# A three-layer decoder kernel: value products of self-attention issued 512 columns wide in every second slot

## The reference

```python
    x = x + _L0_attn_ref(_layernorm(x), W_qkv, b_qkv, W_out, b_out)
    x = x + _L0_xattn_ref(_layernorm(x), ctx_512, ...)
    x = x + _L0_ffn_ref(_layernorm(x), Wg, w1, w2)
# the part of the first that the change touches, for every batch and head (q, k: 512 x 16)
        attn = jnp.einsum('bhqd,bhkd->bhqk', q, k) / jnp.sqrt(HEAD_DIM)
        attn = jax.nn.softmax(attn, axis=-1)
        out = jnp.einsum('bhqk,bhkd->bhqd', attn, v)
```

## Time and profile before

| what | us |
|---|---|
| median of three runs | 1565.12 (1564.07 to 1566.87) |
| the profiled execution | 1563.6 |
| its span, first to last instruction | 1561.8 |
| its A units 0 to 7, from 67.19 to 502.91 | 435.72 |

### The profile page before, as it was taken

How to read it: one execution, slowest core, us unless ns; L and a number is a source line. 1 busy time by engine, 2 the same in 40 slices (tenths; PEclk the granted TensorE clock), 3 DMA queues, 4 the chain that set the end, 5 groups by cost and what they waited for, 6 DMA issues and landing times.

```text
span 1561.8 us, 37676 instructions
## 1 busy us (share of the span) xinstructions
PE 1415.5 (91%) x14538; PEld 634.1 (41%) x14538; DVE 1194.4 (76%) x2434; ACT 1055.4 (68%) x2139; POOL 653.2 (42%) x535
## 2 busy tenths in 40 slices
PE   3799999999999999999999999999899988599997
PEld 1223322332333434434334343343343432279896
DVE  6788888888877777877977878779678785547774
ACT  2387788788778677677676776776767757236562
POOL 2555574466423421336245333362353221235553
PEclk9699999999999999999999999999999999799999
DMA  6435534433323434334333332343334301167771
GB/s 180 128 117 137 147 97 124 133 115 106 94 62 104 111 88 108 91 91 107 87 93 86 105 103 64 91 109 84 84 92 109 84 21 44 42 233 259 271 243 59
DMA packets 119478, 175.80 MB, mean 113 GB/s; under 512 B 26273, under 2 KB 85895, under 8 KB 114696
## 3 DMA queue, kind: packets, MB, share of 16 engines
q1 hardware_dynamic: 111376, 158.50, 35.7%
q0 software_dynamic: 5888, 14.24, 2.8%
q10 hardware_dynamic: 2048, 0.83, 0.2%
HBM read 102.33 MB, written 51.18 MB: 98 GB/s over the span
## 4 chain that ended last, share of the span: by engine, by line
PE 58%; DVE 18%; ACT 8%; DMA 6%; issue 5%; POOL 2%; SPq 1%; DVEq 0%; POOLq 0%; ACTq 0%
PE psO L742 13%; DVE negmax L1221 11%; PE psM L467 11%; PE psS L765 10%; PE psK L467 7%; PE psK L796 6%; ACT probs L1030 6%; PE psS L467 4%; DMA stack<-mrows 3%; DMA recipB<-recip_scratch 2%; PE psK L694 2%; PE psM L832 1%; DVE xn L1169 1%; DVE mrows L1323 1%; PE psM L881 1%
## 5 line engine op out<-in xcount | busy, mean ns | idle before, releaser
L1221 DVE TENSOR_REDUCE negmax<-psS 128x1 f32<-128x512 f32 (+3 forms) x1536 | 868.8, 615 | 222.8 <-PE psS L765 113.4
L1030 ACT ACTIVATE probs<-psK 128x512 f32<-128x512 f32 (+3 forms) x1536 | 755.4, 546 | 309.6 <-PE psK L796 183.9
L742 PE MATMUL psO<-probs,V 128*32 128x256 f32 (+1 forms) x5632 | 440.3, 384 | 10.3 <-ACT U L1022 8.8
L765 PE MATMUL psS<-stack 48*128 48x512 f16 (+3 forms) x1536 | 282.6, 364 | 45.4 <-DVE negmax L1221 41.5
L796 PE MATMUL psK<-stack 50*128 50x512 f16 (+3 forms) x1536 | 276.1, 356 | 17.4 <-DMA stack<-mrows 11.4
L765 PEld LDWEIGHTS psS<-stack 48*128 48x128 f16 x1536 | 74.1, 93 | 357.0 <-DVE negmax L1221 294.9
L742 PEld LDWEIGHTS psO<-probs,V 128*32 128x32 f32 x5632 | 112.3, 108 | 192.2 <-issue 127.8
L1439 POOL TENSOR_TENSOR rstd<-lnt,minus_half 128x4 f32<-128x4 f32 x24 | 24.8, 1033 | 247.1 <-DVE lnt L1161 247.1
L796 PEld LDWEIGHTS psK<-stack 50*128 50x128 f16 x1536 | 75.9, 94 | 49.4 <-issue 17.9
L1571 POOL DMA_INDIRECT out_dram<-stack,put_to x32 | 76.8, 2399 | 17.8 <-issue 9.1
L467 PE MATMUL psM<-xT,wx 128*128 128x512 f16 x288 | 76.7, 382 | 1.6 <-DVE mrows L1323 0.6
(11 more groups left out here) (192 smaller groups left out, 2017.9 us busy)
## 6 DMA issues: line engine op xcount, KB each, us to landing
spare<-in_L_ffn_w_dram SPq DMA_DIRECT2D x32, 1024.0 KB, 6.4
parts_scratch<-parts SPq DMA_DIRECT2D x192, 128.0 KB
stack<-parts_scratch SPq DMA_DIRECT2D x96, 256.0 KB
stack<-parts_scratch SPq DMA_DIRECT2D x96, 128.0 KB
packed<-U SPq DMA_DIRECT2D x192, 64.0 KB
recipB<-recip_scratch SPq DMA_DIRECT2D x48, 256.0 KB
shared<-shared SPq DMA_DIRECT2D x48, 128.0 KB, 2.1
probs<-back_scratch POOLq DMA_DIRECT2D x16, 258.0 KB, 3.2
```

The costliest lines, as they stand in the source:

```text
L742: mm = nc.tensor.matmul(psO[32 * i:32 * i + 32, q0:q1], v_of(par)[:, kt, 2 * g + i % 2 + PAIRS * (i // 2), :], probs[:, (unit + i % 2) % P ...
L765: mm = nc.tensor.matmul(psS[:, banks[hh], 0:n], stack_of(par, 0)[rows, hp, qt * P:(qt + 1) * P], stack_of(par, 1)[rows, hp, 0:n], start=Tr ...
L1030: nc.scalar.activation(probs[:, t % P_RING, i, q0:T], psK[:, S_BANKS[t][i], q0:T], ACT.Exp, scale=SM_SCALE / (1 if b.kind == "A" else WSCA ...
L1221: nc.vector.tensor_reduce(negmax[:, g % 2, at:at + 1], psS[:, S_BANKS[u // 2][j], 0:n], AX_X, ALU.max, negate=True).then_inc(s["max_done"], 1)
```

## The change

In units of kind A, `av(t)` gives nothing in even slots, and in odd slots the whole of the key tile: columns 0 to 511. The same holds for the last groups of an A unit that fall in slots 0 to 2 of the next. `av_done` then counts 16 groups a unit in place of 32. In form "AC" the first load over the old `stack`, which had been in slot 0 and held back by the value products there, moves to slot 1, since slot 0 has none now. Kinds B and C keep the halves.

```diff
     "AC": {"v0": (0,), "v1": (2,), "ctxT0": (7,), "proj0": (10,), "proj1": (11,), "proj2": (14, 15), "proj3": (17, 18),
-           "out0": (22,), "out1": (30,), "load": (0, 3, 3, 6, 7, 9, 9, 10), "split": (8, 10, 12, 15, 18),
+           "out0": (22,), "out1": (30,), "load": (1, 3, 3, 6, 7, 9, 9, 10), "split": (8, 10, 12, 15, 18),
@@ def av(self, t):
         if not kind:
             return None
+        if kind == "A":
+            return (t < 3, (t - 3) % SLOTS, 0, T, True) if t % 2 else None
         half = (t + 1) % 2
         unit = (t - 3 - half) % SLOTS
```

## The result

| what | before | after |
|---|---|---|
| median of four runs each, us | 1565.51 (1564.07 to 1566.87) | 1579.43 (1577.03 to 1581.85) |
| the profiled execution | 1563.6 | 1581.85 |
| its span | 1561.8 | 1580.0 |
| its A units 0 to 7 | 435.7 | 455.2 (67.45 to 522.61) |
| mean granted clock of the span | 0.975 | 0.977 |

The ratio is 1.0095, 95% interval [1.007, 1.0119]: **the change makes the kernel 14 us slower**, 1579.4 where 1580 was forecast. A second series of seven runs of it gave 1.0092 [1.0059, 1.0125].

The account below looks back on a forecast made before the run. TensorE's stream bounds slots with a job, a 1.17 us floor through DVE's reduction those without. Slot pairs sum to +1.6 us a unit, all A units to +15 on the median 1565.1: 1580 us, range 1568 to 1590.

Parts of the forecast that it names:

- The floor: In A units no slot can be shorter than 1.17 us, set by a chain through DVE's reduction of the maxima.
- The rival that the saving of 0.14 a pair counts: TensorE's saving counts after all in A units, every pair of slots giving 0.14 us: 1547 us, chance 0.15.
- The wide group: A value group of 512 columns in A units takes 1.00 us to the next start, 0.43 more than 256 columns.
- the 0.144: Fixed part in us of each group of value products, from a line through groups of 128 and 256 columns.
- The rivals of a cheaper (0.93) and a dearer (1.14) wide group: 512-column value groups in A units: at 0.93 us about 1565 (chance 0.07), at 1.14 us 1598 (chance 0.04).
- The pairs: Odd slot and next even slot of an AA unit, priced by where jobs stand; together +1.6 us a unit.
- The waits for the maxima's rows at a group's start: Exponents waiting for row DMAs at a group's start: taken as nothing, with 2 us if wrong.
- The units: A units: unit 0 +2.2 us, units 1 to 5 +8, unit 6 +1.8, unit 7 +3.2; total +15.
- The bounds of -9 and +9: Range around 1580 us from the 512-column group's time: 0.93 us gives -9, half way to 1.14 gives +9.
- the terms of "slower": Chance of slower by more than 3 us, 0.76: the forecast (0.70), a 512-column group at 1.14 us, and a falling clock.
- The rival of +13 us by the clock: Gaps of up to 0.7 us in some eight odd slots a unit lower the granted clock: 1593 us, chance 0.04.
- What would show it: Signs in the profile after: slot times, waits on DVE, unit 3 at 56 us, kinds B and C within a microsecond.

Follow-up runs that it names:

- the short reductions: Kernel before and changed kernel, each with DVE's reductions and ACT's exponentials of A units over 256 of 512 columns: 1541.3 and 1556.1 us.
- control of the last table: Kernel before, halves in every slot, with a job table that puts both parts of proj0 to proj3 and out0 into two even slots: 1565.45 us.

## Why the prediction was right, and where its terms were off

**The floor.** Slot 9 stayed at 1.17 us, and the short reductions brought such slots to 0.91. The rival that the saving of 0.14 a pair counts (1547) needed this floor to give way. It didn't.

**The wide group** takes 1.00 us to the next start, the value taken. But the reading behind it was half wrong: I called the 0.144 a fixed part of a *group*; the two halves back to back show it as the price of a stretch of value products. The sum doesn't change by that. The rivals of a cheaper (0.93) and a dearer (1.14) wide group fall with the row.

**The pairs.** For unit 3, odd and next even slot together:

| pairs | forecast | measured |
|---|---|---|
| (1,2), (25,26), (31,0) | -0.14 each | -0.17, -0.14, -0.14 |
| (11,12), (15,16), (23,24) | -0.28, -0.21, -0.21 | -0.28, -0.21, -0.21 |
| (9,10), (17,18) | +0.43 each | +0.42, +0.43 |
| (27,28) | +0.29 | +0.36 |
| (13,14), (29,30) | +0.43 each | +0.43, +0.43 |
| (19,20) and (21,22) | +0.2 together | +0.35 together |
| (3,4) | 0 | +0.01 |
| (5,6) and (7,8) | +0.5 together | +0.37 together |
| unit | +1.6 | +1.65 |

Mis-sized were the two terms that I had estimated through ACT's handovers. Of (19) to (22) I had 0.2 and it took 0.35: (19,20) came out at +0.04, since slot 19 stopped at 1.23, and (21,22) at +0.31. Of (5) to (8) I had 0.5 and it took 0.37: (5,6) was the +0.42 expected, while slot 7 gave back 0.68 and slot 8 took 0.63, so (7,8) came to -0.05. That these two errors offset each other, and the unit's sum is so close, is luck.

The waits for the maxima's rows at a group's start, which I had put at nothing, are nothing: the exponents of units 1 to 5 have no idle time in front of them (0.4 us before).

**The units.** Unit 0 +1.8 (forecast +2.2). Units 1 to 5 +7.7 (forecast +8). For unit 6 I had +1.8: outside slot 14 it is +1.3, and with an early load slot 14 adds 0.57, so +1.9; with a late load it adds nothing (4.29 and 4.30). For unit 7 I had +3.2: outside slots 16 to 18 it is +2.9; these add little with a late load, and what they add with an early one no profile shows. Together 1.8 + 7.7 + 1.3 + 2.9 = 13.7, or 14.3 with an early load in unit 6, against 13.9 measured. The sum of the prediction took both units with an early load and had no term for a late one. Over the profiles unit 6 takes 57.5 us with halves and wide alike, and unit 7 takes 54.0 with halves and 58.7 wide. Those means mix the load's time with the change: in the wide profiles the load was the earlier one in unit 6 and the later one in unit 7.

**The range and the chances.** The bounds of -9 and +9 around 1580 are 1571 and 1589, and the terms of "slower" add up to 0.78; the prediction has 1568 to 1590 and 0.76. Nothing rests on the difference.

**The clock.** The rival of +13 us by the clock didn't come: with eleven waits of 0.31 to 0.61 us unit 3 keeps 1.00. It did fall in profiles with longer waits (1.86 us in slot 16 of unit 7, 3.17 in slot 14 of unit 6), to 0.97 over the unit, which is about 1.2 us there (59.40 against 58.18 in unit 7). It did not fall after a wait of 1.76 us in slot 16 of unit 7, nor after one of 2.27 in slot 14 of unit 6 (control of the last table), so the length of one wait doesn't decide it. The Trainium skill, "TensorE: Matmul & The Clock Gate", section "HAM oscillation", tells of short idle stretches that make the clock go up and down; in units 1 to 5 of the changed kernel waits of half a microsecond didn't, and the traces agree only for some of the waits of over a microsecond in units 6 and 7.

**What would show it.** All signs came: 1.00, 1.17, 2.29, 1.29, the longer wait on `mrows` (0.45 for 0.31), unit 3 at 56.0, busy time lower by 2.35, DVE and ACT unchanged. Two were off in size: the idle time of the weight load before slot 10's maxima grew by 0.58 (0.48 to 1.06), not by 0.7. And the units of kinds B and C did move, by 2 us and more in single units and in both directions (unit 8 from 48.80 to 51.09 in one profile and 49.21 in the next), so a microsecond was too narrow a sign; as a whole they take 1058.9 us to the end before (1052.6 in the second profile) and 1057.4 after (1054.2).

## What to carry to other kernels

Where a chain through another engine sets the least time of a step, what counts is each step's own work against that floor, not the engine's total: gather work into every second step only if other work fills the steps it leaves. Merging two instruction groups can save stream and still cost time, by uncovering the handovers that the removed group had filled; list for each removed group who is waited for right behind it, in every place where it stands. And take a second profile of the kernel before where a unit hangs on one DMA's landing, since a single one may show the rare case; then compare slot by slot, for a mean over profiles also holds where the landing fell.

## What the hardware showed that I had not expected

- The fixed part of a float32 value group in four column strips, 0.144 us by the line through two widths, is paid once a stretch: two groups of 256 columns back to back take 1.01 us, one of 512 takes 1.00, two apart 2 x 0.57.
- The same load of `recipB` took 3.75 us from the end of its issue to landing in one profile of the kernel before and 7.39 in the next, in unit 6 of both, and slot 14 went from 2.88 to 7.12 us.
- After a wait of TensorE of 1.76 us in slot 16 of unit 7 the granted clock stayed at 1.00 in one execution, and after 1.86 us in the same slot it fell to 0.50 for 3.41 us in another.
